# Cross-attention and expert FFN on one core: exponentials with a bias per head, two norms merged into one, and q projected a step earlier

## The reference

```python
x = x + xattn(layernorm(x), ctx, ctx, mask, Wq, bq, Wk, bk, Wv, bv, Wo, bo)
    # 16 heads of 16; scores = Q K^T / sqrt(16), masked with -1e9, softmax over the 77 keys, times V, times Wo^T
x = x + ffn(layernorm(x), ...)
    # h = x' + layer_norm(x', ln1) @ attn_w^T, where x' is the argument, itself a norm of x
    # t = layer_norm(h, ln2); the two best of 8 experts by t @ gate_w^T, softmax over the two
    # out = h + sum over the two: weight * down(silu(gate(t)) * up(t))
```

## Time and profile before

| what | value |
|---|---|
| median of 3 runs | 636.17 us (636.09 to 639.53) |
| the profiled execution | 638.29 us |
| its span, first to last instruction | 636.7 us |
| busy: TensorE, VectorE, GpSimd, ScalarE | 536.8, 367.6, 332.6, 250.6 us |
| mean granted TensorE clock | 0.923 of full speed |

### The profile page before, as it was taken

One profiled execution on the slowest core, in us unless ns is written; L12 is line 12 of the kernel. 1 busy time (PEld: TensorE's weight loads), 2 busy tenths in 40 slices (PEclk: granted clock), 3 DMA queues, 4 the chain that ended last, 5 costly groups with the idle time before them and its releaser, 6 DMA issues.

```text
span 636.7 us, 13556 instructions
## 1 busy us (share of the span) xinstructions
PE 536.8 (84%) x3197; PEld 456.7 (72%) x3198; DVE 367.6 (58%) x908; ACT 250.6 (39%) x492; POOL 332.6 (52%) x422
## 2 busy tenths in 40 slices
PE   2579998988998640699999999799999999999960
PEld 1368877776776520588888888688888888888850
DVE  1937889989996458266433436745544643355330
ACT  1145655555554122254332335424334433253210
POOL 4355576767766365375643435664754653346120
PEclk9779999999997555799999999899999999999995
DMA  7760000000000015201221266254154121522123
GB/s 213 239 273 2 33 18 26 26 17 25 25 25 27 17 37 146 84 19 18 41 37 25 33 183 194 60 140 124 26 140 115 26 48 25 172 58 33 17 23 138
DMA packets 27088, 46.57 MB, mean 73 GB/s; under 512 B 9718, under 2 KB 22544, under 8 KB 26768
## 3 DMA queue, kind: packets, MB, share of 16 engines
q1 hardware_dynamic: 15312, 35.77, 17.3%
q0 software_dynamic: 9088, 9.52, 9.3%
q10 hardware_dynamic: 2656, 0.91, 0.7%
HBM read 36.67 MB, written 11.61 MB: 76 GB/s over the span
## 4 chain that ended last, share of the span: by engine, by line
PE 55%; DVE 17%; issue 10%; DMA 8%; POOL 5%; ACT 1%; SPq 0%; DVEq 0%; POOLq 0%; ACTq 0%
PE psum L1174 15%; PE psum L1176 14%; PE psum L1175 14%; PE psum L1205 4%; DMA w_raw<-in_experts 4%; DVE picked L843 3%; DVE s_sb L805 3%; DVE stats L712 2%; PE psum L1056 2%; POOL rstd L492 2%; DMA wk<-in_wkT 1%; POOL s_sb L526 1%; PE psum L1214 1%; PE psum L1107 1%; PE psum L1072 1%
## 5 line engine op out<-in xcount | busy, mean ns | idle before, releaser
L1174 PE MATMUL psum<-w_hi,tb_hi 128*128 x288 | 118.3, 411 | 5.1 <-DVE tb_lo L1012 3.9
L1176 PE MATMUL psum<-w_hi,tb_lo 128*128 x288 | 114.5, 398 | 0.0
L1175 PE MATMUL psum<-w_lo,tb_hi 128*128 x288 | 114.1, 396 | 0.0
L1174 PE MATMUL psum<-w_hi,aT_hi 128*128 x288 | 85.2, 296 | 4.3 <-DVE aT_lo L1000 4.3
L1000 DVE TENSOR_TENSOR aT_lo<-psum,aT_hi 128x512 fp32r<-128x512 f32 x72 | 46.4, 686 | 64.5 <-ACT aT_hi L681 55.2
L1175 PE MATMUL psum<-w_lo,aT_hi 128*128 x288 | 82.2, 285 | 0.0
L1176 PE MATMUL psum<-w_hi,aT_lo 128*128 x288 | 82.1, 285 | 0.0
L576 POOL DMA_INDIRECT acc_rows<-o_sb,add_at x36 | 58.7, 1629 | 33.9 <-POOL add_at L574 33.9
L1006 DVE TENSOR_TENSOR act<-psum,silu 128x512 f32<-128x512 f32 x72 | 49.4, 687 | 33.2 <-PE psum L1176 26.7
L677 ACT ACTIVATE silu<-psum 128x512 f32<-128x512 f32 x36 | 21.6, 600 | 118.7 <-PE psum L1176 115.2
L1174 PEld LDWEIGHTS psum<-w_hi,tb_hi 128*128 128x128 f32 x288 | 55.0, 191 | 17.4 <-issue 7.4
(11 more groups left out here) (170 smaller groups left out, 1099.4 us busy)
## 6 DMA issues: line engine op xcount, KB each, us to landing
w_raw<-in_experts SPq DMA_DIRECT2D x24, 768.0 KB
w_raw<-in_experts SPq DMA_DIRECT2D x2, 3072.0 KB, 13.9
x_sb<-in_x SPq DMA_DIRECT2D x8, 256.0 KB, 5.8
z_rows<-rows SPq DMA_DIRECT2D x16, 128.0 KB
acc_rows<-x_sb SPq DMA_DIRECT2D x16, 128.0 KB, 3.2
ceil_f<-in_mask ACTq DMA_DIRECT2D x2, 308.0 KB, 11.8
blk<-lists POOLq DMA_DIRECT2D x36, 1.0 KB
rows<-z_rows,gather_at POOLq DMA_INDIRECT x36
```

Of the source, the lines that this page charges most:

```text
L1174: nc.tensor.matmul(dst, hi, weights(w_hi, slot, at, cols), start=first, stop=False)
L1175: nc.tensor.matmul(dst, hi, weights(w_lo, slot, at, cols), start=False, stop=False)
L1176: return nc.tensor.matmul(dst, lo, weights(w_hi, slot, at, cols), start=False, stop=last)
```

## The change

1. The subtraction on GpSimd is gone. VectorE writes the negated maximum (s_negmax), and ScalarE takes 16 exponentials per tile, one per head, each with its head's negated maximum as bias. The scale 1/4 goes into qT's eviction (scale SCALE, bias bq_scaled made once), and the mask's ceiling is NEG instead of NEG / SCALE. p_done counts three rounds, after heads 7, 14 and 16, and each round of transposes waits for its own.
2. Norm 2 is merged into norm 1. The variance of xf is var / (var + eps), so the combined root is that of var * (1 + eps) + eps^2. GpSimd makes both roots in one power of two columns, with one more small instruction ahead; VectorE writes z and xf from x1, where ScalarE wrote z from xf. The statistics, moments, root and shift of norm 2 are gone. Norm 3 is now numbered 2.
3. q is projected in the step of the x transposes (t1, a step before the scores): on TensorE between wo and the z transposes, on ScalarE between tT and uT.

The evictions of q stand ahead of uT, xn and the exponentials, which are sixteen. The diff, cut to its core:

```diff
+ROUND_HEADS = [-(-min(4 * (r + 1) * P, SCORES) // KEYS) for r in range(PT_ROUNDS)]
...
@@ gpsimd, inverse_root @@
-                nc.gpsimd.tensor_scalar(var_eps[norm][:, par:par + 1], mv[norm][:, par, 1:2], EPS, None, ALU.add).then_inc(eps[norm], 1)
+                roots = 2 if norm == 1 else 1
+                if norm == 1:
+                    nc.gpsimd.tensor_scalar(var_eps[norm][:, par, 1:2], mv[norm][:, par, 1:2], 1.0 + EPS, EPS * EPS, ALU.mult, ALU.add)
+                nc.gpsimd.tensor_scalar(var_eps[norm][:, par, 0:1], mv[norm][:, par, 1:2], EPS, None, ALU.add).then_inc(eps[norm], 1)
                 pool.wait_ge(eps[norm], number(t) + 1)
-                nc.gpsimd.tensor_tensor(rstd[norm][:, par:par + 1], var_eps[norm][:, par:par + 1], half_neg[:, :], ALU.pow).then_inc(rs[norm], 1)
+                nc.gpsimd.tensor_tensor(rstd[norm][:, par, 0:roots], var_eps[norm][:, par, 0:roots], half_neg[:, 0:roots], ALU.pow).then_inc(rs[norm], 1)
...
@@ gpsimd, tiles @@
-                    inverse_root(3, t6)
-                if within(t5, TILES):
-                    inverse_root(2, t5, z_done)
+                    inverse_root(2, t6)
...
-                if within(t2, TILES):
-                    for part, (h0, h1) in enumerate(((0, FULL_HEADS), (FULL_HEADS, HEADS))):
-                        pool.wait_ge(max_done, 2 * number(t2) + part + 1)
-                        nc.gpsimd.tensor_tensor(s3[:, h0:h1, :], s3[:, h0:h1, :],
-                                                s_max[:, par, h0:h1].unsqueeze(2).to_broadcast([P, h1 - h0, KEYS]),
-                                                ALU.subtract).then_inc(sub_done, 1)
@@ scalar, tiles @@
-                if within(t2, TILES):
-                    act_e.wait_ge(q_ps, number(t2) + 1)
-                    for m in range(KD):
-                        nc.scalar.activation(qT[:, t2[1], m, :], bank[6][:, m * P:(m + 1) * P], ACT.Identity,
-                                             bias=vecs[:, bq_c, m:m + 1]).then_inc(q_done, 1)
...
-                if within(t5, TILES):
-                    norm_apply(2, z[:, t5[1], :], xf[:, t5[1], :], t5, z_done)
...
+                if within(t1, TILES):
+                    act_e.wait_ge(q_ps, number(t1) + 1)
+                    for m in range(KD):
+                        nc.scalar.activation(qT[:, t1[1], m, :], bank[6][:, m * P:(m + 1) * P], ACT.Identity,
+                                             bias=bq_scaled[:, m:m + 1], scale=SCALE).then_inc(q_done, 1)
...
-                        act_e.wait_ge(sub_done, 2 * number(t2) + part + 1)
-                        nc.scalar.activation(p_sb[:, t2[1], c0:c1], s_sb[:, t2[1], c0:c1], ACT.Exp, scale=SCALE).then_inc(p_done, 1)
+                    for h in range(HEADS):
+                        if h in (0, FULL_HEADS):
+                            act_e.wait_ge(max_done, 2 * number(t2) + (h >= FULL_HEADS) + 1)
+                        last = nc.scalar.activation(p_sb[:, t2[1], h * KEYS:(h + 1) * KEYS], s_sb[:, t2[1], h * KEYS:(h + 1) * KEYS],
+                                                    ACT.Exp, bias=s_negmax[:, t2[1], h:h + 1])
+                        if h + 1 in ROUND_HEADS:
+                            last.then_inc(p_done, 1)
@@ vector, tiles @@
-                    norm_apply(1, xf[:, t5[1], :], of(x1_sb, t5), t5, xf_done)
+                    norm_apply(1, z[:, t5[1], :], of(x1_sb, t5), t5, z_done, root=1)
...
-                    dve.wait_ge(xf_done, number(t5) + 1)
-                    norm_stats(2, xf[:, t5[1], :], t5)
+                    norm_apply(1, xf[:, t5[1], :], of(x1_sb, t5), t5, xf_done)
...
-                    norm_moments(2, t5)
...
-                    norm_shift(2, t5)
...
-                    nc.vector.reduce_max(s_max[:, t2[1], h0:h1], s3[:, h0:h1, :], AX_X).then_inc(max_done, 1)
+                    nc.vector.tensor_reduce(s_negmax[:, t2[1], h0:h1], s3[:, h0:h1, :], AX_X, ALU.max, negate=True).then_inc(max_done, 1)
@@ tensor, tiles @@
-                if within(t2, TILES):
-                    pe.wait_ge(xnT_done, number(t2) + 1)
...
-                    last.then_inc(q_ps, 1)
                 if within(t3, TILES):
-                    pe.wait_ge(p_done, 2 * number(t3) + 2)
+                    pe.wait_ge(p_done, PT_ROUNDS * number(t3) + 1)
                     wait_count(pe, pT_done, PT_ROUNDS * number(t3))
                     weights_T(0).then_inc(pT_ps, 1)
+                    pe.wait_ge(p_done, PT_ROUNDS * number(t3) + 2)
...
                     pe.wait_ge(xn_done, number(t1) + 1)
+                    wait_count(pe, q_done, KD * number(t1))
                     transposed(bank[6], xn[:, t1[1], :]).then_inc(xnT_ps, 1)
...
+                    pe.wait_ge(p_done, PT_ROUNDS * number(t3) + 3)
                     weights_T(2).then_inc(pT_ps, 1)
...
                     row_product(bank[7][:, 0:D], oT[:, t4[1], :, :], wo_sb).then_inc(wo_ps, 1)
+                if within(t1, TILES):
+                    pe.wait_ge(xnT_done, number(t1) + 1)
...
+                    last.then_inc(q_ps, 1)
```

More of the change, by code:

```diff
@@ L173, in xattn_moe @@
         stats = sb("stats", [P, 2, 6])
-        mv = [sb(f"mv{i}", [P, 2, 2]) for i in range(4)]
-        var_eps = [sb(f"var_eps{i}", [P, 2]) for i in range(4)]
-        rstd = [sb(f"rstd{i}", [P, 2]) for i in range(4)]
-        shift = [sb(f"shift{i}", [P, 2]) for i in range(4)]
+        mv = [sb(f"mv{i}", [P, 2, 2]) for i in range(3)]
+        var_eps = [sb(f"var_eps{i}", [P, 2, 2]) for i in range(3)]
+        rstd = [sb(f"rstd{i}", [P, 2, 2]) for i in range(3)]
+        shift = sb("shift", [P, 2])
         rows = sb("rows", [P, GATHERS, D])
@@ L647, in tiles @@
                 if within(t0, TILES):
-                    norm_apply(0, xn[:, t0[1], :], of(x_sb, t0), t0, xn_done)
+                    par = t0[1]
+                    act_e.wait_ge(sh_done, number(t0) + 1)
+                    nc.scalar.activation(xn[:, par, :], of(x_sb, t0), ACT.Identity, bias=shift[:, par:par + 1],
+                                         scale=rstd[0][:, par, 0:1]).then_inc(xn_done, 1)
                 if within(t2, TILES):
-                    for part, (c0, c1) in enumerate(((0, FULL_HEADS * KEYS), (FULL_HEADS * KEYS, SCORES))):
-                        act_e.wait_ge(sub_done, 2 * number(t2) + part + 1)
-                        nc.scalar.activation(p_sb[:, t2[1], c0:c1], s_sb[:, t2[1], c0:c1], ACT.Exp, scale=SCALE).then_inc(p_done, 1)
+                    for h in range(HEADS):
[5 more added lines that the diff above has]
+                            last.then_inc(p_done, 1)
             pipeline(act_e, tiles, TILES, LIST, SCATTER)
@@ L716, in norm_moments, with norm_shift, norm_apply @@
                 nc.vector.bn_aggr(mv[norm][:, t[1], :], stats[:, t[1], :]).then_inc(var[norm], 1)
[L718 removed]
+            def norm_shift(t):
                 par = t[1]
+                dve.wait_ge(rs[0], number(t) + 1)
+                nc.vector.tensor_scalar(shift[:, par:par + 1], mv[0][:, par, 0:1], rstd[0][:, par, 0:1], -1.0,
+                                        ALU.mult, ALU.mult).then_inc(sh_done, 1)
+            def norm_apply(norm, dst, src, t, done, root=0):
                 dve.wait_ge(rs[norm], number(t) + 1)
[L721 to L726 removed]
+                nc.vector.tensor_scalar(dst, src, mv[norm][:, t[1], 0:1], rstd[norm][:, t[1], root:root + 1],
                                         ALU.subtract, ALU.mult).then_inc(done, 1)
@@ L1075, in weighted_values @@
                     return done
-                if within(t2, TILES):
-                    pe.wait_ge(xnT_done, number(t2) + 1)
-                    for m in range(KD):
-                        for k in range(KD):
-                            last = nc.tensor.matmul(bank[6][:, m * P:(m + 1) * P], wq_sb[:, k, m * P:(m + 1) * P],
-                                                    xnT[:, t2[1], k, :], start=k == 0, stop=k == KD - 1)
-                    last.then_inc(q_ps, 1)
                 if within(t3, TILES):
-                    pe.wait_ge(p_done, 2 * number(t3) + 2)
+                    pe.wait_ge(p_done, PT_ROUNDS * number(t3) + 1)
                     wait_count(pe, pT_done, PT_ROUNDS * number(t3))
                     weights_T(0).then_inc(pT_ps, 1)
+                    pe.wait_ge(p_done, PT_ROUNDS * number(t3) + 2)
                     if within(t6, TILES):
@@ L1141, in tiles @@
                     row_product(bank[7][:, 0:D], oT[:, t4[1], :, :], wo_sb).then_inc(wo_ps, 1)
+                if within(t1, TILES):
+                    pe.wait_ge(xnT_done, number(t1) + 1)
+                    for m in range(KD):
+                        for k in range(KD):
+                            last = nc.tensor.matmul(bank[6][:, m * P:(m + 1) * P], wq_sb[:, k, m * P:(m + 1) * P],
+                                                    xnT[:, t1[1], k, :], start=k == 0, stop=k == KD - 1)
+                    last.then_inc(q_ps, 1)
                 if within(t5, TILES):
```

50 lines of the change are left out of this document (20 added, 30 removed).

## The result

The changed kernel takes 641.35 us (median of 14 runs, 638.58 to 644.65), the kernel before 637.0 us in the same comparison (14 runs, 634.81 to 641.5). The ratio is 1.0062, 95% interval 1.0038 to 1.0087: slower by 0.6%, where 633 us were forecast. The profiled execution took 641.1 us with a span of 639.5. A ratio leaves out single runs that took longer at a lower granted clock; where they matter, their times and clocks are given.

A forecast was written before the change was run, and what follows sets the result against it. It took VectorE as fullest before and ScalarE's queue, a 10.9 us loop, as the bound after. Fill +6.4, middle -5.5, last tile -1.8 and drain -2.4 gave -3.3 us: 633 us, range 623 to 644.

The forecast's parts named there:

- The exponentials: ScalarE, each tile: sixteen small exponentials, each 0.345 us long and 0.245 apart, the 14th ending after 3.53 us.
- rival of little overlap: ScalarE's exponentials overlap little because each reads another bias; 642 to 653 us, middle 645; chance 0.15.
- The loop: Chain from one tile's first exponential to the next tile's, over TensorE and ScalarE: 10.87 us per step, used as 10.9.
- "picked" and the contention: VectorE's 128x16 product falls from 1751 to about 174 ns once GpSimd's subtraction beside it goes.
- Fill: First steps of the tile phase: scores of tile 6 start at 90.6 instead of 84.24 us, a loss of 6.4.
- fill at a lower clock: Longer pauses keep TensorE at half clock beyond 40 us, two steps, 5 us more, 638 us; chance 0.07.
- Middle: Nine steps from the scores of tile 6 to those of tile 15: 97.6 instead of 103.1 us, a gain of 5.5.
- before the second four transposes: Sign of being right: TensorE idle there about 0.8 us per step, released by the exponentials.
- Last tile: From its scores to its second transposes: 8.4 instead of 10.2 us, a gain of 1.8.
- Drain: After the last tile: shorter waits at "chosen" (1.1), wo (0.7) and later steps; gain 2.4, bounds 0 and 5.
- TensorE as the bound: Rival: exponentials follow faster, so ScalarE's loop does not bind and TensorE's 10.1 us per step does; 622 us; chance 0.2.
- The GpSimd add: Rival: GpSimd's add of h now meets "picked", so contention stays; 6 us, 639 us; chance 0.03.

The follow-up runs named there:

- xn_early: The changed kernel with ScalarE's xn moved from between uT and the exponentials to behind the copies of the first two pT parts; 627.46 us, ratio 0.9807.
- exps_only: The kernel before with only the sixteen exponentials and no GpSimd subtraction, norms and q as before; 620.66 us, ratio 0.9704.
- fill_gap: The changed kernel with five extra TensorE matmuls per step, unread, between the first and second round of p_sb transposes; 629.09 us, ratio 0.9878.
- after_again: The changed kernel itself, nothing altered, executed once more with a profile; 641.57 us.
- q_back: The changed kernel with q and its eviction back at the head of their step, merge and sixteen exponentials kept; 621.7 us, ratio 0.9769.
- q_back_xn: The changed kernel with q back at the head of its step and xn moved behind pT round 1 on ScalarE; 614.81 us, ratio 0.9622.
- q_merge: The kernel before with the merged norm and q one step ahead, GpSimd's subtraction and two exponentials kept; 629.46 us, ratio 0.9853.
- merge_only: The kernel before with only norms 1 and 2 merged, subtraction, two exponentials and q as before; 627.05 us, ratio 0.9836.

## Why the prediction was wrong

**The exponentials** (0.345 us, 0.245 apart, 14 in 3.53 us): right, at 0.358, 0.25 and 3.63 with the hand-over. The rival of little overlap is out. So is the budget of the Trainium skill (ScalarE: Activation LUTs, section Rules for kernel authors) as a sum: its 0.364 us fits the one instruction (0.358), but sixteen in a row took 4.10 us and not 5.8. That the measured 641.35 us lies next to that rival's 642 is a coincidence.

**The loop** (10.87 us): right, 10.84; its parts are in the chain above, and taking xn out of it (xn_early) gave the 0.49 that the sum has for it.

**"picked" and the contention**: right, 165 ns, and also in exps_only.

**Fill** (+6.4, scores of tile 6 at 90.6): with the clock held up 91.3 (fill_gap); in the changed kernel 94.8, since two scores of the fill run at a low clock (3.20 us at 48.7, 4.26 at 60.2). The rival "fill at a lower clock" had this mechanism, with a price of 5 us and only for the fill. Its price was near (94.8 - 91.3 = 3.5; in after_again, whose scores of tile 6 start at 96.4, 5.1), its place too narrow.

**Middle** (-5.5, nine steps in 97.6 us): this is the step that failed. Measured 197.2 - 94.8 = 102.4. Eight steps of 10.9 and one of 10.4 were the sum, and six of the nine are such; three are 12.3 to 12.6, at a low clock. The prediction read 1.00 off the kernel before and carried it over without a term of its own: it put what the clock costs at nothing, for no reason but that row. It costs 4.9 us there (three long scores). The idle time of TensorE "before the second four transposes", which it put at about 0.8 us, is 1.1 to 1.2; the kernel before had 0.73 to 0.97 at a clock of 1.00, so that 0.8 would have been no warning, and what was measured is longer than any gap there was at that place in the middle.

**Last tile** (-1.8): right, 8.67 us where 8.4 were forecast and 10.16 measured before, so -1.5.

**Drain** (-2.4, at most -5): mis-sized. From the last tile's second transposes to the experts' first product it was 61.34 us and is 55.12, so -6.2. The 1.1 counted at "chosen" came (2.11 us after the transposes instead of 3.24), though the wait itself, 1.30, is still 1.23. The wait of wo for oT fell as expected, and the stretch that holds it went from 10.11 to 8.90 us. The big piece is the stretch between: 13.00 us became 9.38, at a clock of 0.84 instead of 0.50, and the sum had no term for the clock here either. In after_again the clock is 0.52, the same stretch takes 12.66, and the drain gains 3.9 instead of 6.2. So 2 to 3 us of the gain go with the clock of one execution and were not earned by the change; what sets the clock there is open.

**Sum.** Forecast +6.4 - 5.5 - 4.2 = -3.3. Measured on the spans, 639.5 - 636.7 = +2.8: scores of tile 15 +9.9, then -7.7, then +0.6 in the experts. With the gap filled the span is 625.4, 14.1 us less: 8.5 up to the scores of tile 15 (197.2 against 188.7), which is what the long scores of fill and middle cost, 3.1 in the drain, where the clock is higher too, and 2.5 in the experts, whose part differs by 3.5 us between the two profiles of the changed kernel. From there to q_back (span 619.3) it is another 6.1: the scores of tile 15 come at 178.9, 9.8 sooner, of which the drain gives back 3.3 (the experts' first product with tb_hi at 249.42 and 242.89) and the experts 0.4. So up to tile 15 the changed kernel is 18.3 us behind q_back, 8.5 by the low clock and 9.8 by longer steps.

**The rivals.** TensorE as the bound (622 us, 0.2) was not this kernel. q_back, the change with q left where it was, takes 621.7, but the equal number is luck: its steps are 10.26 and 10.45, and TensorE still waits 0.44 us in them. With TensorE as the bound (q_back_xn) a step takes 9.77 to 10.02 and the kernel 614.81. The forecast never worked out the change with q left in its place. The GpSimd add did not matter.

## What to carry to other kernels

An idle gap of a microsecond in each step of a TensorE loop has a second price beside its length: the clock may fall behind it, here at a price of 1.7 us each time. When a sum leaves TensorE waiting once per step, give the clock a term, try a few matmuls that nobody reads in the gap, and better, move work that is ready (here q) into it. And weigh each part of a change with the other parts in place: q ahead was free on the old kernel and cost 20 us on the new one.

## What the runs showed of the hardware

- Extra work made the kernel faster: with five matmuls more per step on TensorE 641.35 us became 629.09.
- With equal gaps, a step longer by 0.25 us turned a fall at each third step into one at each second (in the profiled execution, and by time and clock in eight of ten), and one longer by 1.15 us ended them past the fill. What the clock answers to is open; q_merge, meant to part it from the exponentials, missed the gap's length.
- The clock of the drain differs between two executions of the same program: the same stretch took 9.38 us at a granted clock of 0.84 and 12.66 at 0.52.
- One 128x16 product on VectorE costs 165 ns or 1.7 us by what GpSimd does beside it, and 1.02 us when the two overlap in part.
- GpSimd's power of two columns took 0.71 us where that of one takes 0.57, so that the merged norm is cheaper for GpSimd, whose queue, by the waits in its timeline, was the reason for the gain of merge_only in the middle:

```profile
149.83 0.71 POOL L498 TENSOR_TENSOR rstd<-var_eps,half_neg 128x2 f32<-128x2 f32 x1
...
151.26 0.57 POOL L498 TENSOR_TENSOR rstd<-var_eps,half_neg 128x1 f32<-128x1 f32 x1
```
